# A fused hybrid block: splitting the attention maxima on GpSimd, more places for zero products, and a new order of all engines

## The reference, cut to what matters

```
x = x + 0.5 * ffn0(norm(x))      # gate/up/down with blockwise FP4 rounding of activations and weights
x = x + mamba(norm(x))           # in-projection, causal conv of 4 taps, selective scan over 512 tokens, 16 states
x = x + 0.5 * ffn0(norm(x))
x = x + 0.5 * lora(norm(x))      # base linear layer plus 8 gated rank-8 experts
x = x + attention(norm(x))       # 16 heads of 16, causal, with ALiBi bias
x = x + 0.5 * lora(norm(x))
```

```
part0 = bf16(m);  m = m - part0
part1 = bf16(m);  part2 = bf16(m - part1)
```

## Time and profile before

| | |
|---|---|
| Runs, us | 4603.06 / 4607.52 / 4627.58, median 4607.52 |
| Profiled execution: time / span, us | 4599.0 / 4597.2 |
| TensorE busy | 3972.7 us, 86% |
| VectorE busy | 3997.4 us, 87% |
| ScalarE busy | 2376.6 us, 52% |
| GpSimd busy | 1639.1 us, 36% |
| Mean granted TensorE clock | 0.944 of full speed |
| Mean HBM traffic | 163 GB/s |

### The profile page before, as it was taken

One profiled execution on the slowest core, in us unless ns is written; L12 is line 12 of the kernel. 1 busy time (PEld: TensorE's weight loads), 2 busy tenths in 40 slices (PEclk: granted clock), 3 DMA queues, 4 the chain that ended last, 5 costly groups with the idle time before them and its releaser, 6 DMA issues.

```text
span 4597.2 us, 55200 instructions
## 1 busy us (share of the span) xinstructions
PE 3972.7 (86%) x18768; PEld 2065.4 (45%) x18799; DVE 3997.4 (87%) x5964; ACT 2376.6 (52%) x4341; POOL 1639.1 (36%) x1037
## 2 busy tenths in 40 slices
PE   4677788898999899989989999889888888988977
PEld 2233344444545354444535444444544444444443
DVE  6698989998999999899998989899898999988622
ACT  2443454655565555646546465555546554555433
POOL 1153533343434334333433334343443343334100
PEclk9789999999999999999989999999999999999987
DMA  1587886877777787777876876787787787678200
GB/s 60 149 199 188 178 207 146 203 149 186 174 169 191 158 202 168 187 165 176 194 168 172 175 182 161 168 209 160 183 187 180 148 189 177 140 200 184 69 31 23
DMA packets 241438, 753.48 MB, mean 164 GB/s; under 512 B 37650, under 2 KB 132659, under 8 KB 171524
## 3 DMA queue, kind: packets, MB, share of 16 engines
q1 hardware_dynamic: 241156, 749.95, 70.0%
HBM read 647.30 MB, written 101.71 MB: 163 GB/s over the span
## 4 chain that ended last, share of the span: by engine, by line
DVE 41%; PE 31%; DMA 10%; issue 7%; ACT 6%; POOL 2%; SPq 2%; DVEq 0%; ACTq 0%; POOLq 0%
DVE state L1689 12%; DVE u L1684 6%; DVE mt L1786 6%; DMA state<-dtx_scratch 5%; PE m L1178 4%; PE m L1205 3%; PE pd L1399 3%; PE y L1267 2%; PE y L1279 2%; PE m L1220 2%; DVE front L1594 2%; DMA decay<-dt_scratch 2%; DVE front L1623 2%; DVE front L1598 2%; POOL state L784 1%
## 5 line engine op out<-in xcount | busy, mean ns | idle before, releaser
L784 POOL TENSOR_TENSOR state<-state,bc 128x1024 f32<-128x1024 f32 x512 | 1243.7, 2430 | 1606.9 <-DVE u L1684 1604.7
L1689 DVE TENSOR_TENSOR_SCAN state<-decay,u 128x1024 f32<-128x1024 f32 x512 | 1167.1, 2279 | 9.0 <-ACT decay L979 0.6
L979 ACT ACTIVATE decay<-decay,a_neg 128x511 f32<-128x511 f32 x1024 | 675.4, 713 | 219.7 <-DMA decay<-dt_scratch 219.1
L1178 PE MATMUL m<-w_gu,hats_m 128*128 128x480 f32 (+1 forms) x1536 | 710.0, 583 | 60.0 <-DVE front L1598 41.1
L1684 DVE TENSOR_TENSOR u<-state,bc 128x1024 f32<-128x1024 f32 x512 | 649.4, 1268 | 52.9 <-DMA state<-dtx_scratch 41.0
L1267 PE MATMUL y<-state,sel 128*32 128x512 f32 x2048 | 295.1, 652 | 150.3 <-POOL state L784 149.5
L765 POOL TENSOR_TENSOR front<-front,hsc_m 128x704 f32<-128x704 f32 x128 | 189.5, 1481 | 641.6 <-DVE front L1503 641.6
L1178 PEld LDWEIGHTS m<-w_gu,hats_m 128*128 128x128 f32 x1536 | 268.5, 193 | 327.8 <-issue 159.1
L1205 PE MATMUL m<-w_dn,front 128*128 128x256 f32 x1536 | 385.5, 393 | 16.8 <-ACT front L912 16.5
L1125 PE MATMUL y<-minus,zero 128*128 128x512 bf16 x1290 | 334.2, 384 | 0.0
L1205 PEld LDWEIGHTS m<-w_dn,front 128*128 128x128 f32 x1536 | 286.6, 194 | 103.2 <-ACT front L912 51.2
(11 more groups left out here) (263 smaller groups left out, 7163.3 us busy)
## 6 DMA issues: line engine op xcount, KB each, us to landing
decay<-dt_scratch SPq DMA_DIRECT2D x256, 1024.0 KB, 7.4
state<-dtx_scratch SPq DMA_DIRECT2D x256, 1024.0 KB, 11.6
qk_scratch<-shared SPq DMA_DIRECT2D x64, 384.0 KB, 6.0
shared<-qk_scratch SPq DMA_DIRECT2D x384, 64.0 KB
kh<-qk_scratch SPq DMA_DIRECT2D x384, 64.0 KB
xs_scratch<-front SPq DMA_DIRECT2D x16, 1024.0 KB, 12.7
dt_scratch<-front SPq DMA_DIRECT2D x256, 64.0 KB, 3.6
dtx_scratch<-hats_m SPq DMA_DIRECT2D x256, 64.0 KB, 4.2
```

What stands on the lines that cost most here:

```text
L784: eng.tensor_tensor(st, st, bc[:, 1:2, :].to_broadcast([P, WIDE, L]), ALU.mult).then_inc(scan_pool.sem, scan_pool.step(f"c{r}{h}"))
L979: ins = eng.activation(d, d, ACT.Exp, scale=a_neg[:, g:g + 1])
L1178: mm = eng.matmul(f.bank(f"gu{t}{p}")[:, 0:2 * width], norm.hat_t[:, k, t * P:(t + 1) * P], w_gu[:, k, 2 * lo:2 * (lo + width)], start=(k ...
L1689: eng.tensor_tensor_scan(st, decay[:, n % ND, h * WIDE * L:(h + 1) * WIDE * L], u[:, :], 0.0, ALU.mult, ALU.add).then_inc(scan_dve.sem, sc ...
```

## The change

Five edits:

1. `split_maxima` moves from VectorE to GpSimd, unchanged in its four steps and operands. A new semaphore list `att_pool` carries its events. TensorE's `maxima(j)` and VectorE's first reduction of set j+1 now wait on GpSimd.
2. `mine["y"]` is true from the start, so zero products may write `Y` ahead of the first scan.
3. Past the last scan, once ScalarE has read `Y`, one zero matmul opens `Y` again, and zero products may go there to the end.
4. ScalarE's `lead` waits, before it overwrites a normalised-input buffer, for the transposes of the FFN that used that buffer two pieces earlier.
5. The strings of all five engines are new. Digits by kind: SP 2415 and ScalarE 4208, the same counts in another order; GpSimd 1024 to 1280 (digit 2: 192 to 448); VectorE 5792 to 5536 (digit 2: 1760 to 1504); TensorE 6339 to 6647 (digit 5: 1347 to 1654; digit 1: 384 to 385).

```diff
 ORDER = {
...
-        att_dve = Steps(sem("att_dve"), [f"v{t}" for t in range(T)]
-                        + [n for k in range(NG) for n in (scores_of(k) + ([f"m{w}{kind(k)[1]}" for w in "abcd"] if kind(k)[2] == T - 1 else [])
+                        + [n for k in range(NG) for n in (scores_of(k)
                                                          if kind(k)[0] == "s" else []) + [m for w in after_group(k) if w[:2] == "ot" for m in (f"rec{w[2]}", f"att{w[2]}")]])
+        att_pool = Steps(sem("att_pool"), [f"m{w}{j}" for j in range(J) for w in "abcd"])
...
@@ gpsimd: attention
                 yield from rstd(nr, q)
+                def split_maxima(j):
+                    eng.wait_ge(att_dve.sem, att_dve.after(r, f"s{j}{T - 1}{G - 1}"))
+                    if j:
+                        eng.wait_ge(att_pe.sem, att_pe.after(r, f"m{j - 1}"))
+                    elif r:
+                        eng.wait_ge(att_pe.sem, att_pe.after(r - 1, f"m{J - 1}"))
+                    eng.tensor_copy(mt_parts[:, :, 0, :], mt[:, :, :]).then_inc(att_pool.sem, att_pool.step(f"ma{j}"))
+                    yield
+                    eng.wait_ge(att_pool.sem, att_pool.after(r, f"ma{j}"))
+                    eng.tensor_tensor(mt[:, :, :], mt[:, :, :], mt_parts[:, :, 0, :], ALU.subtract).then_inc(att_pool.sem, att_pool.step(f"mb{j}"))
+                    yield
+                    eng.wait_ge(att_pool.sem, att_pool.after(r, f"mb{j}"))
+                    eng.tensor_copy(mt_parts[:, :, 1, :], mt[:, :, :]).then_inc(att_pool.sem, att_pool.step(f"mc{j}"))
+                    yield
+                    eng.wait_ge(att_pool.sem, att_pool.after(r, f"mc{j}"))
+                    eng.tensor_tensor(mt_parts[:, :, 2, :], mt[:, :, :], mt_parts[:, :, 1, :], ALU.subtract
+                                      ).then_inc(att_pool.sem, att_pool.step(f"md{j}"))
+                for j in range(J):
+                    yield
+                    yield from split_maxima(j)
...
@@ scalar: lead, dtx_stored
                             eng.wait_ge(saved, 128 * (WORK[p - 2][1] + 1))
+                    elif p >= 2:
+                        eng.wait_ge(f.pe.sem, f.pe.after(FFNS.index(WORK[p - 2]), "x1"))
...
@@ tensor
-            mine = {"y": False, "pd": False}
+            mine = {"y": True, "pd": False}
...
+                if i == B - 1:
+                    yield
+                    eng.wait_ge(scan_act.sem, scan_act.after(i, "res1"))
+                    eng.matmul(Y[:, 0:P], zero16[:, :], minus16[:, :], start=True, stop=True)
+                    mine["y"] = True
...
                 def maxima(j):
-                    eng.wait_ge(att_dve.sem, att_dve.after(r, f"md{j}"))
+                    eng.wait_ge(att_pool.sem, att_pool.after(r, f"md{j}"))
...
@@ vector: attention
-                def split_maxima(j):
...
                             if t == 0 and g == 0 and j:
-                                eng.wait_ge(att_dve.sem, att_dve.after(r, f"md{j - 1}"))
+                                eng.wait_ge(att_pool.sem, att_pool.after(r, f"md{j - 1}"))
...
-                        if t == T - 1:
-                            yield
-                            yield from split_maxima(j)
```

More of the change, by code:

```diff
@@ L76 @@
     "SP":
[L77 to L84, removed]
@@ L93 @@
[L93 to L94 removed]
+        "00000000000000111000001111000000000000000000111001101111111111111111111111011101100000000000000100000000110000000000010110001111"
+        "11111111111111111111111111111000000000000010101000111000100000000000000011100011221122222222222221212222222222222222111111111222"
@@ new lines @@
+        "22121122222222222212211222222222222122112222221110011000000000000100001111100000000000000001001121001101111111112211222222222222"
+        "22222222122212222222111222222222222222222221112222222222222211122222211100110000000000010000110111000000001000000001001100112110"
+        "11111112211222222222222222222222222222222112221222112222222222222211222222222222221122222211111011000000000000100000111110000000"
+        "00000000000110011211011111112211222222222222222222222222222111222122211122211222222222222221122222222222222112222221110011000000"
@@ new lines @@
+        "00000100000111110000000000000000101011020110111111122112222222222222222222222222222112211222111222122222222222222122222222222221"
+        "21112222221110011000000000000100010111100000000000000000101110201101111111221111222222222222222222222222222222112221112222222222"
+        "22222221122211222222222221122222211100110000000010000011000111000000000000000010011102011011111112211222222222221122222222222222"
+        "22211221111222122222222222221222211122222222222222111222112220000000000000010101001110000000010000000000111001121101111122111122"
@@ new lines @@
+        "22222222222222222222222222221122211122222222222222222111222222222222221122212221110110000000000000100010111100000000000000000010"
+        "01112110111111122112222222222222222222222222222221111222222111222222222222221122222222222222111122222211111000000000000001110000"
+        "11110000000020000000000110001111122111112222222222222222112222222222222211112222221112222222222222211112222222222222211222222011"
+        "10110000000011111100000000111200000000000000000010011011111112211222211222222222222222222222222221111122211222112222222222222211"
@@ new lines @@
+        "22222222222222111222222110000000000000011010001110000000000000000001111200110111111122112222222222222222222222222222221122211111"
+        "22222222222222222112222221212222222112222221110110000000001000000001111100000000000000001101201110011111112211222222222222222221"
+        "22222222222221112222222222222122222221122222222222222112221222111111110000200000000010000101111000000000000000010011120201122222"
+        "22222222222222222222222221122211222112222222222222211222222222222221122212221111111111121111122222222222222222222222222222222222"
```

300 lines of the change are left out of this document (138 added, 162 removed).

## The result

The changed kernel takes 4463.89 us (median of 4 runs, 4447.17 to 4473.65); the kernel before took 4608.82 us beside it (4 runs, 4603.06 to 4627.58). The ratio is 0.9675, with a 95% interval of 0.9634 to 0.9716. The profiled execution has a span of 4466.2 us against 4597.2.

The account below looks back on a forecast made before the run. It took VectorE (92% busy) and TensorE (89%) to bound the middle, and single-step chains at low TensorE clock the ends. Dense part -27, tail -16, head -7 gave -50: 4557 us from 4607.5, range 4508 to 4603.

Parts of the forecast that it names:

- Otherwise I price the moves at nothing, between -20 and +20: All strings: apart from fewer zero products, the new order's shifts of entries were taken as worth 0 us.
- the ends: Head and tail: added zero products raise TensorE's clock; head -7 us, tail -16 us including +4 for splits.
- All of it counts: Rival, chance 0.23: VectorE sets the pace and TensorE waits no longer; -93 us, so 4514 us.
- The dense part gives nothing: Rival, chance 0.17: TensorE behind `maxima` loses as much as VectorE gains; about -12 us, so 4595 us.
- Held GpSimd steps: Rival, chance 0.10: each split step is held behind a VectorE instruction, 4 to 5 us a split; +57, 4665 us.
- The split on VectorE: Four split lines, 56.9 us, leave VectorE; about 50 us in the dense part, priced at -35, between 20 and 50.
- TensorE's wait at `maxima`: TensorE waits 0.9 us longer for the split 30 times: 27 us, half on the path, +13, of which +11 dense.
- GpSimd's price: Four split steps on GpSimd at 0.39 us each: 1.6 us a split, 100 us of GpSimd time in all, hidden.
- -4 for fewer of them between: Dense part: 55 fewer zero products, 12 us of TensorE, times its 31% of the chain: -4 us.
- +4 for the splits: Tail: the last attention has nothing beside its chain, so its four splits cost 0.9 us each, +4.
- 13 us lower: Whole sum by the skill's throttled-time rule, which prices the tail's 86 us at 43 us, not 30.
- What it said would show it: Expected profile signs across VectorE, GpSimd and TensorE, including TensorE's `maxima` wait rising from 24 to about 50 us.

Follow-up runs that it names:

- e9: Changed kernel with the new strings alone: split back on VectorE, zero products at both ends left out; 4528.9 us, 0.9834 of the kernel before.
- e10: Changed kernel with 210 random exchanges of neighbours in VectorE's string, count of adjacent dependent pairs kept at 1238; 4540.1 us.
- e5: Kernel before with neighbours in VectorE's string exchanged so that adjacent dependent pairs fall from 1850 to 1318; 4724.6 us.
- D's runs: Exchanges in VectorE's string testing whether fewer adjacent dependent pairs explain the gain; among them e5, e7, e8 (4724.6, 4537.8, 4684.4 us).
- e2: Changed kernel, new strings kept, with the split put back on VectorE; 4504.9 us.
- e3: Changed kernel without the zero products ahead of the first scan and behind the last; 4482.9 us.
- e7: Changed kernel with neighbours in VectorE's string exchanged so that adjacent dependent pairs fall from 1238 to 1005; 4537.8 us.
- e8: Kernel before, old order with VectorE's string spread by exchanges, plus the split on GpSimd and zero products at both ends; 4684.4 us.

## Why the prediction was wrong

**What failed.** It is the step "Otherwise I price the moves at nothing, between -20 and +20". Measured (e9): 76 to 81 us for the order alone, four times its bound. I had read from the strings that entries stand "10 to 20 us earlier" or "1 to 5 us earlier", and gave no reason for the price of nothing. What an exchange is worth does not follow from its distance: 210 exchanges of neighbours cost 76 us. Of the 95 us that the forecast missed, 72 to 77 are the order beyond the 4 us priced for it, and 22 the split, 41 us for 19; the ends gave about what was forecast.

**Where the time of the order went.** VectorE's time from its first to its last instruction can be split up by all its records: the sum of the durations, less what neighbours overlap, plus gaps under 0.3 us, plus waits over 0.3 us. "Held" is the part of the durations above the median of the instruction's kind, of instructions over 0.1 us above it. Each column is one execution, and how far such sums vary from one to the next isn't known.

| us | before | e9 | changed | e10 | e5 |
|---|---|---|---|---|---|
| sum of durations | 4291.7 | 4250.5 | 4206.4 | 4234.8 | 4320.7 |
| of this held | 88.4 | 55.8 | 50.5 | 84.9 | 124.3 |
| overlap | 331.4 | 349.0 | 353.1 | 344.2 | 358.9 |
| short gaps | 89.1 | 77.8 | 67.7 | 70.5 | 74.7 |
| waits | 530.7 | 550.9 | 531.7 | 569.2 | 664.4 |

From before to changed: durations -85 (57 of them the four split steps with their held casts, most of the other 28 held instructions elsewhere), overlap -22 (more of it), short gaps -21, waits +1; together -127. The changed kernel waits just as long as the one before, with 128 us less in the other terms. That is why the idle time of the scans' stretch is equal, 337 and 335 us. e10 and e5 lose it mainly in two places, waits (+38, +134) and held instructions (+34, +36). For e9 the account gives held -33, overlap -18, short gaps -11, other durations -9, waits +20, together -50: the profiled execution took 4548.2 us, 19 above e9's median, and that of the kernel before 4599.0, some 9 to 16 below its own, so the records show 51 of the 76 to 81 us. How they divide between fewer held instructions, fewer pairs, and waits that didn't grow stays open: no run changed one of the three without the others, and D's runs bought none of them singly by exchanges of neighbours.

**The rivals.** "All of it counts" had the right direction and cause in part: VectorE's busy time in the scans' stretch and the stretch itself fell by the same 110 us. Its 4514 us is still 50 above, since it too priced the moves at nothing. "The dense part gives nothing" had TensorE lose at `maxima` what VectorE gains; TensorE waits less there, 12 us for 24. "Held GpSimd steps" did not come: the means are 251 to 376 ns, below 0.39 us, though the last step's maximum of 1222 ns shows that single ones take over five times their median. The holding that the runs do show is mostly on the other engine: L1531 has two SBUF inputs, and e10's timeline shows it standing until about the end of GpSimd's multiplication. The Trainium skill says (page "SBUF — State Buffer", section "Who interferes with whom") that a VectorE instruction with two SBUF inputs contends with a GpSimd instruction that reads SBUF, and that the order of issue decides which of them is blocked; both orders of the pair agree, 2.81 us for L1531 behind the multiplication and 0.88 ahead of it. L1723, the scan, whose `u` is in PSUM, isn't held: a maximum of 2289 ns for a median of 2278 in e10. I had priced held steps on GpSimd and not read VectorE's string for which multiplications meet its two-input instructions.

**By the other steps.**
- The split on VectorE: -35 + 11 + 1 + 4 = -19 in all forecast, of it 35 for the freed time in the dense part. Measured -15 in the old order and -41 in the new. The two costs that I set against it were TensorE's wait at `maxima` (27 us, +11 on the path) and VectorE's (+1). The first is 12 us for 24 before, the order's doing: by e2 the move itself adds 5 to 6 us, a fifth of the 27. The second is 2.7 us; in the old order it is 19.
- GpSimd's price: 1.6 us a split forecast, 1.21 measured, 77.2 us in all.
- The ends: -20 for the tail's and -7 for the head's products, and -4 for fewer of them between; measured 19 to 28 for both ends. That the distance behind the last scan is 15 us shorter, and 16 were forecast, is in part luck: -20 for the products was too much (16 by e3) and +4 for the splits isn't seen apart. No run shows the -4 by itself. The step from zero products to a higher clock is right: 0.93 for 0.75 and 0.94 for 0.80. By the rule of the Trainium skill that the forecast cited (page "TensorE: Matmul & The Clock Gate", section "Terms") the tail alone would be 43 us; the runs show 19 to 28 for both ends. The rows had TensorE idle for a third of the throttled time, which fits; but some of it stays throttled (0.93), so the two aren't the same quantity. The forecast's "13 us lower" for the whole sum was a slip: 13 is the difference of the upper bounds, 43 and 30, while the sum held -20; with two thirds of 43 it would be 9 lower, with all of it 23.
- What it said would show it: no split lines on VectorE, busy time at least 57 us lower (117 by the page), idle time no more than 15 higher (337 and 335), the end of the last scan some 30 us earlier (116), the clock above 0.9, the last distance 15 us shorter (15). Wrong were the 30, and the wait at `maxima`; GpSimd's 77 us lie just under the 80 to 120.

## What to carry to other kernels

When every engine's order is written out and an edit brings new strings, the strings are the largest edit: don't price them at nothing because each entry moves little, but give them a term and a range of their own (here it was 76 to 81 us), and measure them alone first. Read VectorE's string against GpSimd's: in the one place looked at closely it was better for the instruction with two SBUF inputs to start right behind the one that releases GpSimd's long instruction than 0.3 us after that had begun. The 57 us of instructions taken off the fullest engine were worth most of their time (41) with strings laid out for it, and a quarter (15) in the old ones.

## What the runs showed of the hardware

- A VectorE instruction that needs the result of the one directly ahead starts 35 ns behind that one's end; any other starts 82 ns ahead of it (medians of one kernel). At the 1850 pairs of the kernel before this is 0.2 ms of a 4.6 ms kernel, but taking pairs out by exchanges brought more waits than it saved (e5, e7, e8).
- Where a two-input VectorE instruction meets GpSimd's multiplication, the loss is not shared evenly (one place, e10 and the changed kernel): with VectorE first by 0.17 us, GpSimd's multiplication takes 0.58 us longer; with GpSimd first by 0.29 us, VectorE's takes 1.9 us longer.
- 210 random exchanges of neighbours cost 76 us on VectorE and 46 on TensorE, in a kernel of 4464 us; the 16 us on ScalarE are not clear of noise. 62 and 119 chosen for slack cost nothing that the runs can tell.
- A GpSimd cast or subtraction of 128x16 has means of 0.25 to 0.38 us, and the last step, a subtraction, a median of 0.22 us, against 0.17 us for the subtractions on VectorE.
